# Routing logits of a mixture-of-experts layer: keys held in the array in four column tiles of 32, then one block transpose on VectorE

## What is computed

```python
x = x + attention(layernorm(x))
h = layernorm(x)
# routing: -|h - key|^2 + h @ rw^T + rb for each of 16 experts
logits = -sum((h[:, :, None, :] - keys)**2, -1) + einsum('bld,ed->ble', h, rw) + rb
topv, topi = top_k(logits, 4)
w = softmax(topv)
# experts: w1, gelu, w2 with biases; the 4 chosen ones, weighted by w
x = x + sum(w * expert_out[topi])
```

## Time and profile before

| | us |
|---|---|
| median of 3 runs | 1088.99 (1088.19 to 1089.3) |
| profiled execution, whole | 1082.51 |
| profiled execution, first to last instruction (span) | 1080.6 |
| PE busy | 1047.2 (97%) |
| DVE busy | 839.3 (78%) |
| ACT busy | 828.6 (77%) |
| POOL busy | 681.3 (63%) |

### The profile page before, as it was taken

The page is one execution under the profiler, slowest core; times in us unless marked ns, Lnnn a source line. Parts: engine busy times, 40 slices in busy tenths (PEclk is TensorE's granted clock), DMA queues, the critical chain, the costliest instruction groups (busy, mean ns, idle before and its releaser), DMA issues.

```text
span 1080.6 us, 26984 instructions
## 1 busy us (share of the span) xinstructions
PE 1047.2 (97%) x8355; PEld 848.8 (79%) x8356; DVE 839.3 (78%) x2610; ACT 828.6 (77%) x2040; POOL 681.3 (63%) x902
## 2 busy tenths in 40 slices
PE   8999999999999999999999999999998888999997
PEld 4777777777777777777777777777798878999996
DVE  6888889888888988888898888888665554355587
ACT  5888888888887888888888888877866455776663
POOL 5654554785677568667756766675755665566555
PEclk8999999999999999999999999999999899999999
DMA  7577676677677667776866766787722522222285
GB/s 227 149 210 189 184 210 173 181 203 204 189 192 218 178 188 199 204 198 188 222 178 188 197 177 195 204 264 228 262 77 67 150 72 70 70 71 74 93 261 171
DMA packets 135208, 188.51 MB, mean 174 GB/s; under 512 B 18615, under 2 KB 108480, under 8 KB 135072
## 3 DMA queue, kind: packets, MB, share of 16 engines
q1 hardware_dynamic: 126368, 169.91, 56.6%
q0 software_dynamic: 8704, 16.93, 4.4%
HBM read 100.45 MB, written 87.36 MB: 174 GB/s over the span
## 4 chain that ended last, share of the span: by engine, by line
PE 80%; DVE 5%; POOL 4%; issue 4%; ACT 2%; DMA 2%; another core or an unknown queue 2%; SPq 1%; DVEq 0%; ACTq 0%; POOLq 0%
PE bank L1621 15%; PE bank L1804 12%; PE bank L1674 10%; PE bank L1690 9%; PE bank L1635 9%; PE bank L1701 4%; PE bank L1572 4%; PE bank L1574 4%; PE bank L1573 4%; POOL shared L1029 2%; PE bank L1790 2%; PE bank L1788 2%; PE bank L1789 2%; PE bank L1760 1%
## 5 line engine op out<-in xcount | busy, mean ns | idle before, releaser
L1029 POOL TENSOR_SCALAR shared<-shared,rinv 128x512 f32<-128x512 f32 x512 | 349.0, 693 | 233.8 <-DVE rinv L1300 231.3
L1107 ACT ACTIVATE shared<-shared,nmax 128x512 f32<-128x512 f32 x512 | 368.6, 733 | 72.5 <-DVE nmax L1294 56.9
L1294 DVE CUSTOM_DVE_ANT_0 shared<-bank,shared 128x512 f32<-128x512 f32 x512 | 329.7, 681 | 78.2 <-issue 37.0
L1074 POOL DMA_INDIRECT y_dram<-yb,home x144 | 154.2, 1071 | 109.4 <-issue 88.4
L1313 DVE STREAM_TRANSPOSE turned<-shared 128x512 f32<-128x512 f32 x248 | 160.9, 686 | 1.3 <-issue 1.3
L1804 PE MATMUL bank<-shared,act_h 128*128 x1152 | 146.6, 282 | 14.3 <-DVE yb L1460 11.4
L409 POOL DMA_INDIRECT xs_dram<-copies,slot x128 | 133.9, 1046 | 40.8 <-issue 29.8
L1113 ACT ACTIVATE pt_e<-bank 128x512 f32<-128x512 f32 x256 | 144.8, 594 | 17.2 <-PE bank L1635 15.4
L1804 PEld LDWEIGHTS bank<-shared,act_h 128*128 128x128 f32 x1152 | 137.7, 196 | 20.4 <-issue 20.3
L1635 PE MATMUL bank<-idn,shared 128*128 128x128 f32 x1024 | 137.1, 276 | 0.5 <-DVE nmax L1294 0.5
L1635 PEld LDWEIGHTS bank<-idn,shared 128*128 128x128 f32 x1024 | 112.6, 141 | 24.2 <-issue 16.9
(11 more groups left out here) (245 smaller groups left out, 1880.7 us busy)
## 6 DMA issues: line engine op xcount, KB each, us to landing
pt_dram<-turned SPq DMA_DIRECT2D x496, 128.0 KB
pt_d<-pt_dram SPq DMA_DIRECT2D x124, 512.0 KB
xb<-xs_dram SPq DMA_DIRECT2D x64, 130.0 KB
shared<-in_experts SPq DMA_DIRECT2D x16, 514.0 KB
yk_sb<-y_dram SPq DMA_DIRECT2D x24, 256.0 KB
shared<-roll_dram SPq DMA_DIRECT2D x3, 768.0 KB, 8.5
y_dram<-yb,home POOLq DMA_INDIRECT x144
xs_dram<-pad_sb SPq DMA_DIRECT2D x17, 130.0 KB
```

The lines of the kernel that those rows point to most:

```text
L1029: pool.tensor_scalar(tile, tile, rinv[:, 2 * v + hh:2 * v + hh + 1], 1.0, ALU.mult, ALU.mult)\
L1074: pool.indirect_dma_start(y_dram, bass.IndirectOffsetOnAxis(ap=home[:, j, c:c + 1], axis=0), yb[:, j, c, :], None, bounds_check=last_row, ...
L1107: act.activation(prob[:, v, hh, :], prob[:, v, hh, :], ACT.Exp, bias=nmax[:, n:n + 1], scale=-1.0, accum_out=rsum[:, n:n + 1]).then_inc(ex ...
L1294: dve.tensor_tensor_reduce(prob[:, v, hh, :], score_bank(v, hh)[:], strips[:, 2 * i + hh, v * P:v * P + S], -1.0, BIG, ALU.add, ALU.min, n ...
```

## The change

The stationary operand and the streamed one change places. `rk` is widened from 16 to 32 columns (BK = P // TC = 32), the added ones zero, and is loaded as the stationary operand of four array tiles of 128 rows by 32 columns. Tile a gets, as its moving operand, the tokens whose number within a chunk lies in 32a to 32a+31, of all four chunks: 128 columns in four runs of 32. So the result has, on partitions 32a to 32a+31, the experts, and 4 x 32 tokens along the free axis. One block transpose on DVE (32 by 32 blocks, 128 by 128 in all) turns it to tokens on partitions and writes it to `lg_t` in SBUF; the addition of `lconst` then reads `lg_t`, not the bank. `lg_rdy` counts two a batch now: DVE waits for its own transpose before the addition, and PE's wait for the bank is for the transpose.

```diff
@@ route_pe, stage 1
-                for c in range(TC):
-                    mm = pe.matmul(to[:, c * NE:(c + 1) * NE], xt[:, c * P:(c + 1) * P], rk[:], start=True, stop=True)
+                tokens = xt[:].rearrange("d (c a r) -> d a c r", c=TC, r=BK)
+                for a in range(P // BK):
+                    mm = pe.matmul(to[a * BK:(a + 1) * BK, 0:TC * BK], rk[:], tokens[:, a], start=True, stop=True)
@@ route_dve, stage 4
-                dve.tensor_tensor(lg[:], route_bank(n)[:, 0:TC * NE].rearrange("p (c e) -> p c e", e=NE),
-                                  lconst[:].unsqueeze(1).broadcast_to([P, TC, NE]), ALU.add).then_inc(lg_rdy, 1)
+                dve.transpose(lg_t[:].rearrange("p c e -> p (c e)"), route_bank(n)[:, 0:TC * BK]).then_inc(lg_rdy, 1)
+                dve.wait_ge(lg_rdy, 2 * n + 1)
+                dve.tensor_tensor(lg[:], lg_t[:, :, 0:NE], lconst[:].unsqueeze(1).broadcast_to([P, TC, NE]), ALU.add)\
+                    .then_inc(lg_rdy, 1)
             elif stage_no == 5:
-                dve.wait_ge(lg_rdy, n + 1)
+                dve.wait_ge(lg_rdy, 2 * n + 2)
@@ routing_constants, once in step (0, 1)
-                    dve.scalar_tensor_tensor(rk[:], keys_sb[:], 2.0, rw_sb[:], ALU.mult, ALU.add).then_inc(rk_rdy, 1)
+                    dve.memset(rk[:, NE:BK], 0.0).then_inc(rk_rdy, 1)
+                    dve.scalar_tensor_tensor(rk[:, 0:NE], keys_sb[:], 2.0, rw_sb[:], ALU.mult, ALU.add).then_inc(rk_rdy, 1)
@@ aside_taken, and the same in block_pe for the last batch
-                        pe.wait_ge(lg_rdy, b)
+                        pe.wait_ge(lg_rdy, 2 * b - 1)
```

More of the change, by code:

```diff
@@ L113, in layer_kernel @@
         keys2 = sb("keys2", [P, NE])
-        rk = sb("rk", [P, NE])
+        rk = sb("rk", [P, BK])
         lrow = sb("lrow", [P, NE])
@@ L136, in layer_kernel @@
         row_of = sb("row_of", [P, NLATE])
+        lg_t = sb("lg_t", [P, TC, BK])
         lg = sb("lg", [P, TC, NE])
@@ L1730, in aside_taken @@
                 if (b, i) == (0, 3):
-                    pe.wait_ge(rk_rdy, 1)
+                    pe.wait_ge(rk_rdy, 2)
                     pe.wait_ge(bf_rdy, 1)
@@ L1813, in block_pe @@
                     if TAIL_PE[m] == 2:
-                        pe.wait_ge(lg_rdy, NB)
+                        pe.wait_ge(lg_rdy, 2 * NB - 1)
                     route_pe(pe, LAST, TAIL_PE[m])
```

## The result

| | before | after |
|---|---|---|
| median, us | 1088.53 (1087.17 to 1089.3, 6 runs) | 1081.95 (1081.59 to 1085.03, 6 runs) |
| ratio, with its 95% interval | | 0.994 (0.992 to 0.9961) |
| profiled execution, us (span) | 1082.51 (1080.6) | 1085.03 (1083.2) |

The changed kernel is faster by 6.6 us (4.2 to 8.7 by the interval), where 3.6 were forecast.

What follows compares the result with a forecast made beforehand. PE's own instruction list was taken to bound attention, and weight loading the changed block. Savings of 7 x 0.50 + 0.13 = 3.6 us off 1088.99 gave 1085.4 us, range 1083.8 to 1089.4.

Steps and rivals of the forecast that it cites:

- PE's own list passes on one for one: In attention, PE is busy throughout a step, so 0.50 us cut from its list shortens each (b,3) step by that.
- L361 is bound by weight loading: Old logits block: 8 fp32 loads of 128 columns, about 0.11 us each, set its 1.00 us.
- How many tiles at once: New logits block in steps (b,3): 0.42 us with four tiles at once, 0.63 with two; 0.50 taken, saving 0.50 in seven steps.
- The last batch: Logits block in block 7, between whole-array neighbours: 0.50 plus 0.17 us for entry, 0.67 in place of 0.80, saving 0.13.
- VectorE 0.33 to 0.39 us for the addition, hidden: DVE's added transpose and wait, eight times, cost 0.33 to 0.39 us each, covered by at least 1.04 us of idle.
- DVE has no idle left at that place: Sign of failure: no DVE idle before the first score of step (b,4), where about 0.3 us was expected, from 1.22.
- second cover: PE's quarter-3 scores, which wait for DVE's queue, start 2.2 us into the next step, leaving 0.4 us more room.
- The waits for L429 still two: Sign in the profile after: PE still waits twice for DVE's normalised tokens from L429, 0.9 us in two before.
- the gain is given back by waits: Rival, chance 0.20: five more attention steps wait 0.46 us each, 2.3 us back, 1087.7; batch 7 could hold on to 0.5.
- Tiles not side by side: Rival, chance 0.12: the new logits block's tiles run in turn, 1.06 us a block, 0.85 us slower, 1089.8.
- loads not hidden: Rival, chance 0.07 shared with DVE the bound: load and streaming in turn, 1.93 us a block, 7.8 us slower, 1096.8.
- DVE the bound: Rival, chance 0.07 shared with loads not hidden: DVE 0.5 us dearer than taken; each further 0.1 us costs 0.7.

Runs made afterwards that it cites:

- chips 12 and 6: The change measured again, twice, against the kernel before, both with a free SyncE count edit: ratio 0.9948 (5.5 us by the ratio), then 0.9966 (3.6 us).
- the third measurement: The change once more against the kernel before, both with a free SyncE count edit: 1046.64 us against 1050.34, ratio 0.9966 (0.9953 to 0.9979).

## Why the prediction was off in size

The mechanism, the sign and the place were right; the size was not. Step by step:

- *PE's own list passes on one for one.* Right where nothing waits: (1,3) lost 0.65 us, as its block did. The doubled old block gave 5.3 to 6.1 of 7.1 us. All in all PE's list got 4.8 us shorter, and the kernel 3.6 to 5.5 us faster on chips 12 and 6.
- *L361 is bound by weight loading.* Right: 0.89 us for a second one, 8 x 0.111.
- *How many tiles at once: the term "I take 0.50".* Mis-sized, and the main miss. It took a place between two and four tiles at once for the passes (0.30 us), and 0.20 us for entry and exit. All four run at once (0.22 us for 8 records), which is 0.08 of the miss. The other 0.06 is entry and exit: 0.14 in place of 0.20. The 0.20 was made of 0.17 for entry, read behind L356, which is not the neighbour here; the entry lies in the 1.88 us ahead of the block, before and after alike, so it was no term of the difference. The block is 0.36; that is 7 x 0.14 = 1.0 us more saved than forecast, and below the end of 0.42 that was to hold it.
- *The last batch, "0.67 us in place of 0.80".* Mis-sized in the same way: from the first L1764 to L363 it is 0.31 us, where it was 0.22 to L361, so the entry costs 0.09 and not 0.17, and the block itself is 0.36. It saves 0.36 us, not 0.13; the text had 0.21 as the most. Together with the term before it is 4.8 in place of 3.6.
- *VectorE 0.33 to 0.39 us for the addition, hidden.* The size holds nearly in six of eight batches (0.32 from the transpose to the addition, and 0.33 from there to L455, where it was 0.32 before), and hidden it is: 1.0004. What I missed is that the addition moves from PSUM to SBUF for its source and so collides with POOL's normalisation: 0.46 us more in the steps (1,3) and (7,3), and in four of the others the next instruction with both operands in SBUF (L461) takes 0.56 to 0.60 in place of 0.16. So the idle of at least 1.04 us was used up, not left at 0.3: it is gone in six of the seven steps and 0.07 in the last, and in step (1,3) the first score starts 1.17 us into the next step, where it was 1.10. "DVE has no idle left at that place" was named as a sign of failing; it came, and it cost nothing that the runs could measure. I had the scores' distance (2.2 us) as a second cover; doubling the part showed that it holds for most of it.
- *The waits for L429 still two.* They are three here, 1.1 us in place of 0.9, and three in the other two profiles of the change.
- *Rival "the gain is given back by waits"*, 0.20. It happened in part. From the start of step (1,0) to that of (7,7) the two profiles of before take 655.5 and 654.2 us and the three of the change 653.1, 652.2 and 652.3: 2.3 us less by their means, where the seven blocks are 4.5 us shorter. A tenth of the gain goes in one place. The stretch from the step's start to L357 is 8.24 us in step (2,3) and 8.19 in (5,3), where before it is 8.00 in both; that is 0.43 us, and within 0.01 of it in all three profiles of the change. PE's shorter block isn't needed for it: the kernel that has only DVE's part has 8.25 in (2,3). But DVE's part isn't enough either: with that part twice, with one tile of 128 and with two of 64 it is 8.00 to 8.01 in (2,3). Where it shows first in (2,3) is this pair of rows, the fifth score, 4.22 us after the step's start before and 4.57 after:

```profile
242.08 0.69 DVE L1294 CUSTOM_DVE_ANT_0 shared<-bank,shared 128x512 f32<-128x512 f32 x1 [0.52 <-PE bank L1635]
```

```profile
241.15 0.69 DVE L1297 CUSTOM_DVE_ANT_0 shared<-bank,shared 128x512 f32<-128x512 f32 x1 [0.86 <-PE bank L1639]
```

  POOL's normalisations stand at the same 3.34 us of the step in both, and PE's transposes that release this score as well, so what the score waits for is not what the view names. The cause stays open.
- *Waits for `pt_d`.* 1.7 us in the profile of before and 1.4 in its repeat; 4.0, 3.7 and 2.8 in the three of the change. Each profile is one execution, and with other kernels that have a short block they were between 1.6 and 5.2; with the long block of one tile of 128 they were 3.1. So that an earlier PE meets this transfer more often is likely, not shown. Together with the 0.43 this could account for a gain below 4.8, such as the 3.6 of the third measurement; no run separates it.
- *Tiles not side by side; loads not hidden; DVE the bound.* None of them happened: 1.06 is what one tile gives, and the load of 108 ns hides behind streaming of 108.
- *The range.* Its low end stood on a block of 0.42 and on two waits that vanish, which they didn't: the largest gain in it is 5.2 us. PE's list got shorter by 4.8, which lies inside. The 1.8 us beyond that, of the 6.6 measured, are inside the measurement's own interval (4.2 to 8.7), and chips 12 and 6 gave 3.6 to 5.5. In the result's runs both kernels also carry the stalls of the expert blocks, which vary (287.0 and 292.3 us in the two profiled executions). Whether some of the 1.8 us is real there wasn't shown, and I put it down to nothing: with the block's right size the forecast would have been 1084.2, inside the range, and still 2.2 us above what was measured.

## What to carry to other kernels

A small product that is bound by loading its stationary side gains nothing from exchanging the operands alone; it gains when the narrow operand, now stationary, lets the array be split into column tiles, here from 0.86 to 0.22 us for the streaming alone. Price such a block from its neighbours in the list, and leave out of the difference what the old block pays as well: a change of tiling costs 0.09 to 0.14 us on either side here, so that half as many tiles in the neighbours' own tiling can come out even. And when an edit moves an operand from PSUM to SBUF, look at what GpSimd reads at that moment.

## What the runs showed of the hardware

- Four fp32 column tiles of 32 run fully side by side, both passes: a second group of 8 records of 128 columns costs 0.22 us, against 0.86 in turn. In a single block the first four records start within 0.02 us and the eight within 0.15. The Trainium skill says in "TensorE: Matmul & The Clock Gate", section "Part 3: Packing small matmuls", that packed matmuls start a few ns apart and overlap; the trace agrees, with four starts within 0.02 us.
- The same 16 records take 1.74 us up to the next start when the next block keeps the tiling, and 1.88 when it does not.
- A 128 x 128 fp32 block transpose on DVE takes 288 ns out of PSUM (316 in the kernel with VectorE's part alone) and 312 ns out of SBUF, as a plain operation of that size does (320 ns with an addition, out of PSUM).
- A DVE addition with both operands in SBUF is held until a normalisation of POOL that also reads SBUF ends: 0.69 us in place of 0.23. With one operand in PSUM it is not: 0.23, begun 0.03 to 0.05 us behind such a normalisation, in seven steps.
- The same kernel took 1088.5 us in the result's runs and 1050.3 to 1052.0 on three chips of the experiments, with most of the difference in the expert blocks (287.0 against 257.3 us). There, at times, no engine is busy: 3.4 us in sum in the first, none in the second. Whether it is the chip, which the result's record doesn't name, or something else, and what makes the engines stand, wasn't shown.
